# Attention scores from two float32r parts in the two row halves of TensorE, in place of three bf16 parts

## The reference, cut to what matters

```python
q, k, v = split_heads(x @ Wq + bq), split_heads(x @ Wk + bk), split_heads(x @ Wv + bv)   # x layer-normed
scores = jnp.einsum('bhid,bhjd->bhij', q, k)
rel = jnp.einsum('bhid,pd->bhip', q, rel_key)                   # p = 256
bias = take_along_axis(rel, clip(j - i + p - 1, 0, p - 1), axis=3)
logits = jnp.where(j <= i, (scores + bias) * hd ** -0.5, -inf)
out = softmax(logits) @ v
x = x + layernorm(out @ Wo + bo)
x = x + layernorm(ffn(layernorm(x)))
```

## Time and profile before

| what | value |
|---|---|
| median of 3 runs | 739.25 us (734.71 to 739.43) |
| the profiled execution | 737.71 us |
| its span, first to last instruction | 735.6 us |
| PE busy | 645.0 us, 88% |
| ACT busy | 572.5 us, 78% |
| DVE busy | 538.9 us, 73% |
| mean granted TensorE clock | 0.947 of 2.4 GHz |

### The profile page before, as it was taken

One profiled execution on the slowest core, in us unless ns is written; L12 is line 12 of the kernel. 1 busy time (PEld: TensorE's weight loads), 2 busy tenths in 40 slices (PEclk: granted clock), 3 DMA queues, 4 the chain that ended last, 5 costly groups with the idle time before them and its releaser, 6 DMA issues.

```text
span 735.6 us, 18944 instructions
## 1 busy us (share of the span) xinstructions
PE 645.0 (88%) x8066; PEld 467.9 (64%) x8066; DVE 538.9 (73%) x923; ACT 572.5 (78%) x660; POOL 246.6 (34%) x175
## 2 busy tenths in 40 slices
PE   4877669999999999999999999978799898998993
PEld 2333336676766766867667667655588687786682
DVE  5885787787687877786877777765677568588546
ACT  2794977988989889889898898786577868677573
POOL 2100270360640912705408128010271441731801
PEclk9988767999999999999999999997999999999997
DMA  7487423152241231521412314040300000000001
GB/s 229 113 228 219 134 84 90 38 129 66 51 111 40 71 96 35 130 69 43 106 52 68 100 34 123 27 158 1 101 1 1 0 1 1 1 29 0 6 24 59
DMA packets 39175, 52.82 MB, mean 72 GB/s; under 512 B 5656, under 2 KB 29640, under 8 KB 36680
## 3 DMA queue, kind: packets, MB, share of 16 engines
q1 hardware_dynamic: 39088, 51.58, 25.6%
HBM read 39.00 MB, written 11.81 MB: 69 GB/s over the span
## 4 chain that ended last, share of the span: by engine, by line
PE 53%; DVE 13%; ACT 12%; issue 5%; POOL 2%; DVEq 0%; ACTq 0%; POOLq 0%
PE p_o L1114 16%; PE p_s L1089 13%; PE p_z L1788 8%; PE p_z L1791 8%; DVE probs L1215 6%; ACT probs L1332 6%; PE p_s L1023 5%; POOL hid_lo L1709 1%; DVE res L1969 1%; ACT hid_hi L1892 1%; ACT o_acc L1341 1%; ACT even_b L1036 1%; ACT odd_b L1036 1%; PE p_o L1126 1%; DVE hid_lo L1993 1%
## 5 line engine op out<-in xcount | busy, mean ns | idle before, releaser
L1089 PE MATMUL p_s<-q_sb,k_sb 96*128 96x128 bf16 (+1 forms) x1600 | 172.2, 250 | 9.2 <-ACT probs L1332 3.5
L1332 ACT ACTIVATE probs<-p_s 128x1024 f32<-128x1024 f32 x160 | 156.6, 1017 | 18.5 <-DVE p_s L1224 10.8
L1114 PE MATMUL p_o<-probs,v_sb 128*32 128x128 f32 (+1 forms) x3200 | 159.7, 331 | 7.5 <-ACT o_acc L1341 4.7
L992 POOL TENSOR_SCALAR_AFFINE_SELECT even_b<-even_b 128x2048 f32<-128x2048 f32 x31 | 75.9, 2449 | 259.6 <-ACT even_b L1036 259.6
L1332 ACT ACTIVATE probs<-probs 128x1024 f32<-128x1024 f32 x128 | 133.5, 1055 | 36.1 <-DVE probs L1215 35.8
L1089 PEld LDWEIGHTS p_s<-q_sb,k_sb 96*128 96x128 bf16 x1600 | 113.9, 100 | 68.5 <-issue 30.3
L1215 DVE TENSOR_TENSOR probs<-p_s,even_b 128x1024 f32<-128x1024 f32 x96 | 114.9, 1218 | 16.8 <-PE p_s L1089 16.8
L1114 PEld LDWEIGHTS p_o<-probs,v_sb 128*32 128x32 f32 x3200 | 84.6, 111 | 40.9 <-issue 13.9
L1788 PE MATMUL p_z<-hid_hi,h_hi 128*128 128x512 f32 x256 | 102.1, 399 | 1.7 <-POOL hid_lo L1709 1.7
L1023 PE MATMUL p_s<-q_rows,rel_w 72*128 72x64 bf16 x2048 | 83.8, 196 | 19.6 <-DVE probs L1215 8.7
L1791 PE MATMUL p_z<-hid_lo,h_hi 128*128 128x512 f32 x256 | 100.9, 394 | 0.0
(11 more groups left out here) (182 smaller groups left out, 846.2 us busy)
## 6 DMA issues: line engine op xcount, KB each, us to landing
k_sb<-k_dram SPq DMA_DIRECT2D x48, 192.0 KB
q_sb<-q_dram SPq DMA_DIRECT2D x16, 576.0 KB
q_rows<-qr_dram SPq DMA_DIRECT2D x42, 192.0 KB
q_dram<-q_parts SPq DMA_DIRECT2D x12, 256.0 KB, 3.0
k_dram<-k_parts SPq DMA_DIRECT2D x12, 256.0 KB, 3.2
qr_dram<-q_turned SPq DMA_DIRECT2D x12, 256.0 KB, 3.4
x_all<-in_L_attn_x_dram SPq DMA_DIRECT2D x4, 512.0 KB, 4.4
every<-in_L_ffn_h_w_dram SPq DMA_DIRECT2D x2, 1024.0 KB, 8.3
```

Of the source, the lines that this page charges most:

```text
L992: nc.gpsimd.affine_select(out=far, in_=near, compare_op=ALU.is_ge, fill=0.0, base=-1 - r, pattern=[[0, QB], [-1, MCH * RCH]], channel_mult ...
L1089: last = nc.tensor.matmul(slot[:, c:c + n * BLK], k_sb[hg][:, h * S + j * BLK:h * S + (j + 1) * BLK], ap(q_sb[hg], at, [[HG * S, KROWS], [ ...
L1114: last = nc.tensor.matmul(p_o[32 * h:32 * h + 32, at:at + blocks * BLK], v_sb[hg][:, j, h * 32:(h + 1) * 32], probs[n % PBUFS][:, h, col * ...
L1332: nc.scalar.activation(to, got, ACT.Exp, scale=SCALE).then_inc(t_exp, 1)
```

## The change

q and k are split into two parts with 12 bits each (float32r) instead of three bf16 parts: 4 products x 8 channels are 32 rows, with the bound 34. `k_sb` and `q_sb` hold one head of a step in partitions 0 to 33 and the other in partitions 64 to 97, and the matmuls of the two heads alternate. The ones in `k_sb` come from two memsets on POOL, so that the padding and its DMAs go. The turned query for the bias stays in three bf16 parts, but is now made from `qf` directly: ACT writes its high part in the turned order, DVE subtracts in that order, and the third `turn_query` goes. `k_rest` and the third part of k go. The heads of a step become h and h + 2 of a group of four; DVE's and PE's views follow. The stores are float32. The diff, cut to its core (the branch that isn't taken follows in the same way):

```diff
 ROWS = PARTS * PARTS * HD
-KROWS = 96
+SPLIT = 2
+GROUP = 64
+PROWS = SPLIT * SPLIT * HD
 EPS = 1e-5
...
 MPARTS = 2
-EVEN_REST = 144
-STORED_ROOM = 5184
+SROWS = PROWS + MPARTS
+EVEN_REST = 656
+STORED_ROOM = 4160
 FIRST_BEFORE = 4
...
-    q_dram = nc.dram_tensor("q_dram", [PARTS, HD, B * H, S], BF16, kind="Internal")
+    q_dram = nc.dram_tensor("q_dram", [SPLIT, HD, B * H, S], F32, kind="Internal")
...
-    k_dram = nc.dram_tensor("k_dram", [HD, PARTS, B * H, S], BF16, kind="Internal")
-    m_dram = nc.dram_tensor("m_dram", [MPARTS, B * H, S], BF16, kind="Internal")
+    k_dram = nc.dram_tensor("k_dram", [HD, SPLIT, B * H, S], F32, kind="Internal")
+    m_dram = nc.dram_tensor("m_dram", [MPARTS, B * H, S], F32, kind="Internal")
...
-    rel_w = sb("rel_w", [KROWS, P + BLK], BF16)
+    rel_w = sb("rel_w", [ROWS, P + BLK], BF16)
...
-    q_sb = [sb(f"q_sb{p}", [KROWS, HG * S], BF16, operands) for p in range(2)]
+    q_sb = [sb(f"q_sb{p}", [2 * GROUP, HPS * S], F32R, operands) for p in range(2)]
...
-    k_sb = [sb(f"k_sb{p}", [KROWS, HG * S], BF16, operands) for p in range(2)]
+    k_sb = [sb(f"k_sb{p}", [2 * GROUP, HPS * S], F32R, operands) for p in range(2)]
...
-    qf, kf, q_rest, k_rest = (sb(n, [128, S], F32, one) for n in ("qf", "kf", "q_rest", "k_rest"))
+    qf, kf, q_rest = (sb(n, [128, S], F32, one) for n in ("qf", "kf", "q_rest"))
...
+    q_hi, k_hi = (sb(n, [128, S], F32R, one) for n in ("q_hi", "k_hi"))
...
-    q_parts, k_parts = (sb(n, [128, PARTS, S], BF16, one) for n in ("q_parts", "k_parts"))
-    m_parts = sb("m_parts", [H, MPARTS, S], BF16, one)
+    q_lo, k_lo = (sb(n, [128, S], F32R, one) for n in ("q_lo", "k_lo"))
+    m_parts = sb("m_parts", [H, MPARTS, S], F32R, one)
...
         at = (u * 2 + hg) * (HG * S)
-        sp.dma_start(q_sb[hg][0:ROWS, :], ap(q_dram, at,
-                     [[DROW, PARTS * HD], [0, PARTS], [1, HG * S]])).then_inc(t_q[hg], 16)
+        for x in range(2):
+            sp.dma_start(q_sb[hg][x * GROUP:x * GROUP + PROWS, :].bitcast(F32),
+                         ap(q_dram, at + x * (HPS * S), [[DROW, SPLIT * HD], [0, SPLIT], [1, HPS * S]])).then_inc(t_q[hg], 16)
     def load_m(u, hg):
         at = (u * 2 + hg) * (HG * S)
-        sp.dma_start(q_sb[hg][ROWS:ROWS + MPARTS, :], ap(m_dram, at,
-                     [[DROW, MPARTS], [1, HG * S]])).then_inc(t_q[hg], 16)
+        for x in range(2):
+            sp.dma_start(q_sb[hg][x * GROUP + PROWS:x * GROUP + SROWS, :].bitcast(F32),
+                         ap(m_dram, at + x * (HPS * S), [[DROW, MPARTS], [1, HPS * S]])).then_inc(t_q[hg], 16)
     def load_k(u, hg):
-        own = PARTS * HD
-        for copy in range(PARTS):
-            sp.dma_start(k_sb[hg][copy * own:(copy + 1) * own, :],
-                         ap(k_dram, (u * 2 + hg) * (HG * S), [[DROW, own], [1, HG * S]])).then_inc(t_k[hg], 16)
+        own = SPLIT * HD
+        at = (u * 2 + hg) * (HG * S)
+        for x in range(2):
+            for copy in range(SPLIT):
+                row = x * GROUP + copy * own
+                sp.dma_start(k_sb[hg][row:row + own, :].bitcast(F32),
+                             ap(k_dram, at + x * (HPS * S), [[DROW, own], [1, HPS * S]])).then_inc(t_k[hg], 16)
...
-        for p in range(2):
-            for rows, dst, which in ((ROWS + MPARTS, q_sb[p], 0), (ROWS, k_sb[p], 1)):
-                n = KROWS - rows
-                sp.dma_start(ap(dst, rows * (HG * S), [[HG * S, n], [512, HG * S // 512], [1, 512]]),
-                             ap(pads, which * 512, [[2 * 512, n], [0, HG * S // 512], [1, 512]])).then_inc(s_pads, 16)
-        sp.wait_ge(s_pads, 16 * 4)
...
-
-        def store(b, to, rows, part, got, done):
-            sp.dma_start(ap(to, rows[0] * part + b * (H * S), [[S, H], [rows[1], HD], [1, S]]),
-                         got[:, part, :]).then_inc(done, 16)
-
-        def turned(b, part):
-            sp.wait_ge(s_turned, b * PARTS + part + 1)
-            store(b, qr_dram, (HD * DROW, DROW), part, q_turned, s_rst)
...
+
+        def store(b, to, part, rows, got, done):
+            sp.dma_start(ap(to, part + b * (H * S), [[S, H], [rows, HD], [1, S]]), got).then_inc(done, 16)
+
+        def turned(b, part, made):
+            sp.wait_ge(made, b + 1)
+            store(b, qr_dram, part * (HD * DROW), DROW, q_turned[:, part, :], s_rst)
+
+        def split(b, part, made, q, k, done):
+            sp.wait_ge(made, b * 2 + 1)
+            store(b, q_dram, part * (HD * DROW), DROW, q[:, :].bitcast(F32), done)
+            sp.wait_ge(made, b * 2 + 2)
+            store(b, k_dram, part * DROW, SPLIT * DROW, k[:, :].bitcast(F32), done)
...
             if b == 1:
-                for done in (s_qst, s_kst, s_rst):
-                    sp.wait_ge(done, 16 * PARTS)
+                sp.wait_ge(s_hst, 16 * 2)
+                sp.wait_ge(s_lst, 16 * 2)
+                sp.wait_ge(s_rst, 16 * PARTS)
                 sp.dma_start(q_rows[:, :], ap(qr_dram, 0, [[DROW, PARTS * HD], [0, PARTS], [1, UH * S]])).then_inc(t_qr[0], 16)
                     load_q(0, hg)
-            for part, made in enumerate((s_hi, s_mid, s_low)):
-                sp.wait_ge(made, b * 2 + 2)
-                store(b, q_dram, (HD * DROW, DROW), part, q_parts, s_qst)
-                store(b, k_dram, (DROW, PARTS * DROW), part, k_parts, s_kst)
-                if not last:
-                    turned(b, part)
+            turned(b, 0, s_thi)
+            split(b, 0, s_hi, q_hi, k_hi, s_hst)
+            turned(b, 1, s_tmid)
+            split(b, 1, s_lo, q_lo, k_lo, s_lst)
+            if not last:
+                turned(b, 2, s_tlow)
         batches(batch)
         shift(B - 1)
-        for part in range(PARTS):
-            turned(B - 1, part)
-        sp.wait_ge(s_qst, 16 * PARTS * B)
+        turned(B - 1, 2, s_tlow)
+        sp.wait_ge(s_hst, 16 * 2 * B)
+        sp.wait_ge(s_lst, 16 * 2 * B)
         sp.wait_ge(s_rst, 16 * PARTS * B)
-        sp.wait_ge(s_kst, 16 * PARTS * B)
         sp.wait_ge(s_mst, 16 * B)
...
-        step(nc.gpsimd.memset(rel_w[64:KROWS, :], 0.0), 3)
+        step(nc.gpsimd.memset(k_sb[0][:, :].bitcast(F32), 1.0), 3)
...
-        nc.gpsimd.memset(pads[:, 0, :], 0.0)
-        step(nc.gpsimd.memset(pads[:, 1, :], 1.0), 9)
+        step(nc.gpsimd.memset(k_sb[1][:, :].bitcast(F32), 1.0), 9)
...
-        def low_q(b):
-            dve.wait_ge(s_mid, b * 2 + 1)
-            nc.vector.tensor_tensor(q_parts[:, 2, :], q_rest[:, :], q_parts[:, 1, :], ALU.subtract).then_inc(s_low, 1)
-
-        def low_k(b):
-            dve.wait_ge(s_mid, b * 2 + 2)
-            nc.vector.tensor_tensor(k_parts[:, 2, :], k_rest[:, :], k_parts[:, 1, :], ALU.subtract).then_inc(s_low, 1)
+        def rest_q(b):
+            dve.wait_ge(s_thi, b + 1)
+            nc.vector.tensor_tensor(q_rest[:, :].rearrange("p (r i) -> p r i", i=NB), untouched_view(qf), turned_view(q_turned, 0),
+                                    ALU.subtract).then_inc(s_rest, 1)
+
+        def low_parts(b):
+            dve.wait_ge(s_hi, b * 2 + 1)
+            dve.wait_ge(s_lst, b * (16 * 2))
+            nc.vector.tensor_tensor(q_lo[:, :], qf[:, :], q_hi[:, :].bitcast(F32), ALU.subtract).then_inc(s_lo, 1)
+            dve.wait_ge(s_hi, b * 2 + 2)
+            nc.vector.tensor_tensor(k_lo[:, :], kf[:, :], k_hi[:, :].bitcast(F32), ALU.subtract).then_inc(s_lo, 1)
+
+        def low_turned(b):
+            dve.wait_ge(s_tmid, b + 1)
+            nc.vector.tensor_tensor(q_turned[:, 2, :], q_rest[:, :], q_turned[:, 1, :], ALU.subtract).then_inc(s_tlow, 1)
...
                 biased_v(b)
-            dve.wait_ge(s_hi, b * 2 + 1)
-            nc.vector.tensor_tensor(q_rest[:, :], qf[:, :], q_parts[:, 0, :], ALU.subtract).then_inc(s_rest, 1)
-            dve.wait_ge(s_hi, b * 2 + 2)
-            nc.vector.tensor_tensor(k_rest[:, :], kf[:, :], k_parts[:, 0, :], ALU.subtract).then_inc(s_rest, 1)
+            rest_q(b)
+            low_parts(b)
             if not last_batch:
                 biased_v(b)
-                low_q(b)
-                low_k(b)
+                low_turned(b)
             if b == CHECKS:
...
-        low_k(B - 1)
...
-        dve.wait_ge(s_low, B * 2)
+        dve.wait_ge(s_lo, B * 2)
...
             if not first:
-                act.wait_ge(s_turned, b * PARTS)
-                act.wait_ge(s_qst, b * (16 * PARTS))
-                act.wait_ge(s_kst, b * (16 * PARTS))
-            nc.scalar.activation(q_parts[:, 0, :], qf[:, :], ACT.Identity).then_inc(s_hi, 1)
+                act.wait_ge(s_rst, b * (16 * PARTS))
+            nc.scalar.activation(turned_view(q_turned, 0), untouched_view(qf), ACT.Identity).then_inc(s_thi, 1)
+            if not first:
+                act.wait_ge(s_hst, b * (16 * 2))
+            nc.scalar.activation(q_hi[:, :], qf[:, :], ACT.Identity).then_inc(s_hi, 1)
             act.wait_ge(s_kf, b + 1)
-            nc.scalar.activation(k_parts[:, 0, :], kf[:, :], ACT.Identity).then_inc(s_hi, 1)
-            if not last_batch:
```

(49 more changed lines are left out.)

62 lines of the change are left out of this document (28 added, 34 removed).

## The result

The changed kernel takes 880.96 us (median of 4 runs, 856.02 to 926.52) against 739.34 for the kernel before in the same job. The forecast was 729, its range ended at 793. The profiled execution took 867.6 us, its span is 865.8, 130 us more than before.

A forecast was written before the change was run, and what follows sets the result against it. PE was taken to bound stage two, busy 46.5 of 49.3 us a unit. 737.71 less 6 (stage one) and 4 (stage two) gave 727.7; with the median 1.5 above the profiled execution, 729 us, range 712 to 793.

The forecast's parts named there:

- at a full granted clock of 1.00: Stage two: PE's clock read from the earlier trace as 1.00 (2.4 GHz), with 49.3 us a unit.
- Stage two at the full clock: Stage two: PE net 0.8 us less a unit, times 0.62 and 8 units, 4 us less.
- A further 4 x 256 step: Stage two scores: halves load and stream beside each other, so a 4 x 256 step takes 0.22 us, 0.23 less.
- A step of 8 x 128: Stage two scores: the load of 104 ns bounds each pair, so the step stays at 0.42 to 0.45 us.
- The changes of form: Stage two, PE: switching into and out of the scores' form, with uncovered first loads, costs 4.0 us a unit.
- Stage one: Before the first exponentials: fewer conversions and turned writes give 6 us less, between 2 and 9.
- Step (2): Stage one, batch 2: after its store wait ACT has fewer turned writes and conversions, 4.6 us less.
- Step (3): Stage one, after the table load: three turned writes leave ACT and low_k leaves DVE, 1.3 us less.
- no earlier than 105: Sign of failure: first exponentials no earlier than 105 us if stage one's DMA wait grew; near 101.5 if right.
- (1): Rival, stage two: weight loads of the two halves go one behind the other; 789 us, 770 to 810; chance 0.24.
- (2): Rival, stage two: halves don't stream at the same time, but loads hide; 753 us, 742 to 765; chance 0.15.
- (3): Rival, stage two: no cost for change of form, some gain in the 128s too; 715 us; chance 0.15.

The follow-up runs named there:

- e1: The changed kernel with 64 rows instead of 34 in each half, the added rows zeros in q and ones in k: 747.9 us, ratio 1.0145.
- e5: The kernel before, bf16 and full form, with score matmuls reading only the first 34 of 96 rows: 855.91 and 819.91 us.
- e10: e1 with q and k in two bf16 parts instead of float32r, the remainder left out of the scores: 719.49 us, ratio 0.9756.
- e11: The kernel before with its scores in bf16 row halves of 64 rows, two smallest products left out, stage one unchanged: 718.53 us, ratio 0.9727.
- e7: e1 with zeros written by DMA and POOL's masks held until after the last batch's own product: 745.41 us, ratio 1.0094.
- e9: e7 with the last batch's q_lo and k_lo moved behind DVE's opening copies: 751.38 us, ratio 1.0189.
- e3: e1's layout and types, but each score matmul over all 128 rows, so the two heads are summed and nothing overlaps: 791.84 us.
- e4: The changed kernel, 34 rows, with all matmuls of one head of a step before those of the other: 944.39 us.
- e2: The kernel before with score matmuls reading 74 rows instead of 96, leaving out the zero padding: 742.0 us.
- e8: The kernel before with POOL's masks held until DVE has written the last batch's own product: 739.51 us, ratio 1.0006.

## Why the prediction was wrong, point by point

**The step that failed** is the one behind every number of stage two: "at a full granted clock of 1.00", read from the earlier trace rows and then carried over to a kernel whose score matmuls use 34 rows instead of 96. Each rival priced PE's work at that clock as well; none had the clock in it. What the runs showed in its place is a clock of 0.50 for 185 us on end. They put 114 of the 122 us there (861.8 to 747.9 with zeros in the empty rows, e1), and show the low clock with bf16 in the full form too (e5).

**Stage two at the full clock, 4 us less forecast.** Measured over 7.5 units it is 1.2 less (366.6 in e1 for 367.8). At the same clock it is nearer nothing, as the kernel before stood at 1.2 GHz for some 7 us of that stretch (0.91 in 160 to 180 us, 0.97 in 420 to 480) and e1 for none. The single unit shown has 49.8 us where 48.8 was forecast and the earlier trace rows has 49.3. The parts:
- A further 4 x 256 step: 0.22 forecast, 0.25 measured. Right: streams and loads of the halves do overlap. But in the unit shown only one such step stands directly behind another (461.94); the lone ones went from 0.45 to 0.43 only.
- A step of 8 x 128: 0.42 to 0.45 forecast, 0.56 behind another of its kind, and 0.42 or 0.56 behind a 4 x 256. This term was mis-sized for most. I took 104 ns for a pair, as if the two loads hid each other wholly; a pair takes 140. (0.8 ns a column makes 102 or 103 ns, not 104; nothing hangs on it.) There are 12 such steps, so at most 12 x 0.14 = 1.7 us a unit. With bf16 loads a lone step takes 0.33 (e10, e11), so it is the load that bounds it.
- The changes of form, 4.0 us a unit forecast from halves of the column form's price. A lone 4 x 256 step costs 0.18 more than a further one in float32r and 0.10 in bf16: the 0.08 between them fits the uncovered load (0.09 forecast), and the 0.10 the change, though no run takes them apart. In a lone step of 8 x 128 it hardly shows (0.59 for 0.56). The bias chunk costs 0.11 more ahead of scores, and the transposes 0.15. These two were set at 0.05; they are two to three times that, and in e11's bf16 too (there a chunk ahead of scores takes 0.57 as well).

**Stage one, 6 us less forecast.** Step (2), `qf(3)` 4.6 us earlier, measured 5.1. Step (3), "what is late then is DVE's last copy, just before 106.19", was wrong in its hidden assumption that DVE's work keeps its durations. It moved beside POOL's masks and was stretched; `q_rest`, which now reads and writes in the turned order, takes 1.98 and in the last batch 2.85 us instead of 1.22. The first exponentials came at 105.55, which the prediction had named as its own sign of failure ("no earlier than 105"), though for another reason: ACT's wait for the stores did end earlier (70.85), as one of the bounds had it. And the earlier exponentials did not show in the time: the first output came at 130.5 instead of 126.2, as PE got its full clock back at 128 us instead of 118. What was still to be won there is not settled: e7 and e9 moved the collision, and their first outputs came at 131.7 and 132.7, behind the same late clock.

**The rivals.** (1) is what happens without overlap (e3, 792 for 789) and is not this kernel. (2) falls with the 0.25. (3) is not this kernel either: there is a cost of the change of form, and the 128s gain with bf16 loads only (e10, e11). The loads of operands and SP's extra issues cost nothing that shows: from 120 to 500 us PE waits for none of them in the changed kernel, in e1 and, with twelve issues, in e11.

## What to carry to other kernels

Before making a matmul smaller in its contracted rows, ask what clock it will be granted: here a kernel lost 114 us by using 34 rows and got them back from zeros in rows left idle. The busy share does not show this; read the granted clock beside it, by stretch, and compare it between two runs before a difference of a few microseconds is put down to the code (e9). And change one thing at a time: here the row halves were worth 20 us with bf16 loads (e11), and the wide parts that came in the same edit took them back: 13 us in stage two and 9 ahead of it (e1 against e11).

## What the runs showed of the hardware

- The granted clock of TensorE fell to 1.2 GHz for 185 us and more (235 to 420) with PE busy in all of it. By rows of the score matmuls, in windows of 60 us from 120 to 480: 34 in each half 0.50 to 0.98 (e4: 0.50 in all); 48 in each half 0.86 to 1.00; 64 in each half in float32r 0.90 to 0.92 in the first window and 1.00 behind it (e1, e7, e9), in bf16 0.94 to 1.00 (e10, e11); full form, 34 rows 0.50 to 1.00, 74 rows 0.91 to 1.00, 96 rows 0.97 to 1.00, 128 rows in float32r 1.00. Zeros in q with ones in k served as well as data.
- At the start of stage two the full clock came back at 116 to 118 us in the kernel before, e2, e3, e8, e10 and e11, and at 129 to 132 in e1, e7 and e9, float32r in halves of 64 rows. Why is open.
- Loads into the two row halves overlap, but not wholly when they are wide: a further pair of 128 columns takes 140 ns in float32r (105 in one place of a unit), and 240 ns when each covers the full array; in bf16 four pairs take 0.33 us, about 80 ns a pair with the change of form in it.
- Some DVE operations from SBUF were stretched by POOL's masks on 2048 columns: two of 64 columns from 0.42 to 4.72 us (two masks of 2.36), a subtraction of 1024 from 1.2 to 3.3 us. Reductions of 1024 columns beside a mask kept 1.20.
